# Cross-attention on one core: row maxima transposed on VectorE in 32x32 blocks, weight-by-value products in two blocks of four quads, four exponential buffers

## The reference, cut to what matters

```python
q = apply_axial_rope(q, pos_map)
k = apply_axial_rope(k, ctx_pos_map)
logits = jnp.einsum('bqhd,bkhd->bhqk', q, k) * scale
w = jax.nn.softmax(logits, axis=-1)
attn = jnp.einsum('bhqk,bkhd->bqhd', w, v)
```

## Time and profile before

| | |
|---|---|
| timed runs | 456.71 us median of 3 (454.82 to 458.28) |
| span of the profiled execution | 458.8 us |
| PE busy | 359.8 us (78%) |
| DVE busy | 244.2 us (53%) |
| ACT busy | 211.2 us (46%) |
| POOL busy | 167.2 us (36%) |

### The profile page before, as it was taken

How to read it: one execution, slowest core, us unless ns; L and a number is a source line. 1 busy time by engine, 2 the same in 40 slices (tenths; PEclk the granted TensorE clock), 3 DMA queues, 4 the chain that set the end, 5 groups by cost and what they waited for, 6 DMA issues and landing times. The chain is left out here.

```text
span 458.8 us, 9423 instructions
## 1 busy us (share of the span) xinstructions
PE 359.8 (78%) x3050; PEld 213.1 (46%) x3050; DVE 244.2 (53%) x654; ACT 211.2 (46%) x394; POOL 167.2 (36%) x241
## 2 busy tenths in 40 slices
PE   0545989999999999999999759876998898766000
PEld 0432546666666666666565424453546643322000
DVE  6364546766666676666767344799784430111000
ACT  2232557667666666666667375441662321111000
POOL 9144214442234443224300020242387142667730
PEclk9995899999999999999999857999999998697555
DMA  8896356101111000111320023411043787222245
GB/s 206 257 251 186 102 143 203 26 9 29 29 29 29 24 17 18 29 29 25 89 59 2 2 95 117 166 24 46 1 123 114 220 237 193 22 28 26 26 79 116
DMA packets 35036, 39.28 MB, mean 86 GB/s; under 512 B 8032, under 2 KB 29120, under 8 KB 34752
## 3 DMA queue, kind: packets, MB, share of 16 engines
q1 hardware_dynamic: 24082, 21.55, 16.5%
q10 hardware_dynamic: 8030, 11.93, 9.0%
q0 software_dynamic: 2896, 5.44, 7.0%
HBM read 26.36 MB, written 10.32 MB: 80 GB/s over the span
## 5 line engine op out<-in xcount | busy, mean ns | idle before, releaser
L469 DVE TENSOR_REDUCE mx<-bank 128x4 f16<-128x512 f32 x128 | 88.2, 690 | 45.6 <-PE bank L571 43.0
L364 ACT ACTIVATE pw<-bank 128x512 f32<-128x512 f32 x128 | 76.7, 599 | 56.8 <-PE bank L584 56.7
L244 POOL TENSOR_TENSOR rot<-t 128x256 f32<-128x256 f32 x30 | 21.2, 727 | 131.6 <-DVE t L462 131.6
L571 PE MATMUL bank<-kz,qst 128*128 128x512 f16 x128 | 50.6, 397 | 5.8 <-DMA kz<-kT 5.7
L597 PE MATMUL bank<-pw,V 128*32 128x128 f32 x1024 | 54.8, 286 | 0.1
L584 PE MATMUL bank<-qst,kz 128*128 128x128 f16 x512 | 50.1, 221 | 4.2 <-DMA qst<-mxs 4.2
L584 PEld LDWEIGHTS bank<-qst,kz 128*128 128x128 f16 x512 | 37.8, 99 | 14.6 <-issue 5.8
L597 PEld LDWEIGHTS bank<-pw,V 128*32 128x32 f32 x1024 | 20.2, 108 | 31.9 <-issue 30.4
L1171 PE MATMUL mbank<-hT,WSG 128*128 128x512 f16 (+1 forms) x144 | 32.6, 384 | 0.0
L873 POOL DMA_INDIRECT out<-ac,dst x16 | 21.7, 1355 | 29.6 <-DVE ac L1114 10.4
L1114 DVE TENSOR_SCALAR ac<-mbank,wpair 128x256 f32<-128x256 f32 x16 | 7.7, 484 | 45.7 <-DMA odd<-ac,dst 42.8
(11 more groups left out here) (174 smaller groups left out, 659.4 us busy)
## 6 DMA issues: line engine op xcount, KB each, us to landing
ring_gu<-in_L_ffn_w_gate_up ACTq DMA_DIRECT2D x20, 352.0 KB
kz<-kT SPq DMA_DIRECT2D x64, 64.0 KB, 2.0
ring_dn<-in_L_ffn_w_down ACTq DMA_DIRECT2D x10, 352.0 KB
ring_gu<-in_L_ffn_w_gate_up SPq DMA_DIRECT2D x8, 352.0 KB
X<-in_x SPq DMA_DIRECT2D x4, 512.0 KB, 7.3
table<-ac SPq DMA_DIRECT2D x8, 256.0 KB, 2.1
odd<-zero SPq DMA_DIRECT2D x1, 2048.0 KB, 7.0
out<-X SPq DMA_DIRECT2D x4, 512.0 KB, 3.1
```

The costliest lines, as they stand in the source:

```text
L244: eng.tensor_tensor(rot[:, part], t1[:, part], t2[:, part], ALU.add).then_inc(rot_ok[w], 1)
L364: act.activation(pw[g % 2][:, :], STB[g % 2][:, :], ACT.Exp, scale=SCALE).then_inc(exp_ok, 1)
L469: dve.tensor_reduce(mx[u // 2 % 2][:, :, u % 2], SB[u % 2][:, :].rearrange("p (j t) -> p j t", j=4), axis=AX.X, op=ALU.max, negate=True).t ...
L571: pe.matmul(SB[u % 2][:, :], qst[m.par][:, u, :], kz[m.par][:, :, u, :], start=True, stop=True).then_inc(s_mm, 1)
```

## The change

- `mx` becomes a tile of 128 x 32, of which 8 columns are written, the rest is zeroed once. DVE transposes it in 32x32 blocks straight into `mxs` (also 128 x 32). Each group of 32 tokens then has its 8 rows of maxima in its own 32 partitions. The PE transpose, its semaphore `mxT_mm`, and the copy from PSUM are gone.
- SP copies each half into `qst` with four DMAs, one for each group of 32 tokens (8 rows of 32 values), in place of one (8 rows of 128 values).
- `weigh_values` is called in two blocks: in step 4 for quads 0 to 3 of b, and in step 0 for quads 4 to 7 of b-1. Before, each step had one quad.
- The exponentials go to four buffers `pw`, so that four can wait.

```diff
                         sp.wait_ge(mxs_ok, k + 1)
-                        sp.dma_start(qst[who.par][MAXROW:P:SLOT, 2 * half:2 * half + 2, :],
-                                     mxs[half % 2][:, :]).then_inc(mr_in[half % 2], 16)
+                        for c in range(4):
+                            sp.dma_start(qst[who.par][MAXROW:P:SLOT, 2 * half:2 * half + 2, 32 * c:32 * c + 32],
+                                         mxs[half % 2][32 * c:32 * c + 8, :]).then_inc(mr_in[half % 2], 16)
...
-                        at_least(act, pv_mm, QUADS * b.n + g - 1)
-                        act.activation(pw[g % 2][:, :], STB[g % 2][:, :], ACT.Exp, scale=SCALE).then_inc(exp_ok, 1)
+                        at_least(act, pv_mm, QUADS * b.n + g - 3)
+                        act.activation(pw[g % 4][:, :], STB[g % 2][:, :], ACT.Exp, scale=SCALE).then_inc(exp_ok, 1)
...
-            def evac_max(m, half):
-                k = 4 * m.n + half
-                dve.wait_ge(mxT_mm, k + 1)
-                at_least(dve, mr_in[half % 2], 16 * (2 * m.n + half // 2))
-                dve.tensor_copy(mxs[half % 2][:, :], SB[1][0:8, 0:P // 2].bitcast(F16)).then_inc(mxs_ok, 1)
+            def turn_max(m, half):
+                dve.wait_ge(max_ok, QUADS * m.n + 2 * half + 2)
+                at_least(dve, mr_in[half % 2], 64 * (2 * m.n + half // 2))
+                dve.transpose(mxs[half % 2][:, :], mx[half % 2][:, :]).then_inc(mxs_ok, 1)
...
-            def transpose_max(m, half):
-                pe.wait_ge(max_ok, QUADS * m.n + 2 * half + 2)
-                pe.transpose(SB[1][0:8, 0:P // 2].bitcast(F16), mx[half % 2][:, :, :], identh[:, :]).then_inc(mxT_mm, 1)
...
-                    if g % 2 == 1:
-                        who, half = (b, (g + 3) // 2) if g < 5 else (m1, (g - 5) // 2)
-                        if inside(who):
-                            transpose_max(who, half)
...
                     if g == 0 and inside(o):
-                        weigh_values(o, QUADS - 1)
-                    if g > 0 and inside(b):
-                        weigh_values(b, g - 1)
+                        for q in range(4, QUADS):
+                            weigh_values(o, q)
+                    if g == 4 and inside(b):
+                        for q in range(4):
+                            weigh_values(b, q)
```

More of the change, by code:

```diff
@@ L179, in attention @@
         V = [sb(f"V{i}", [P, NH, SLOT]) for i in range(2)]
-        mx = [sb(f"mx{i}", [P, 4, 2], F16) for i in range(2)]
-        mxs = [sb(f"mxs{i}", [8, P], F16) for i in range(2)]
-        pw = [sb(f"pw{i}", [P, 4 * P]) for i in range(2)]
+        mx = [sb(f"mx{i}", [P, SLOT], F16) for i in range(2)]
+        mxs = [sb(f"mxs{i}", [P, SLOT], F16) for i in range(2)]
+        pw = [sb(f"pw{i}", [P, 4 * P]) for i in range(4)]
         OT = [sb(f"OT{i}", [P, 4, P]) for i in range(2)]
@@ L204, in attention @@
         consts, consts2, kz_zero = sem("consts"), sem("consts2"), sem("kz_zero")
+        mx_zero = sem("mx_zero")
         stat1, mv1_ok, std1, rs1_ok = sem("stat1"), sem("mv1_ok"), sem("std1"), sem("rs1_ok")
@@ L213, in attention @@
         v_mm, v_ok = sem("v_mm"), sem("v_ok")
-        s_mm, max_ok, mxT_mm, mxs_ok = sem("s_mm"), sem("max_ok"), sem("mxT_mm"), sem("mxs_ok")
+        s_mm, max_ok, mxs_ok = sem("s_mm"), sem("max_ok"), sem("mxs_ok")
         mr_in = [sem(f"mr_in{i}") for i in range(2)]
@@ L415, in _ @@
                                       ALU.mult, ALU.add).then_inc(turn_s, 1)
+            for i in range(2):
+                dve.memset(mx[i][:, :], 0.0).then_inc(mx_zero, 1)
             dve.wait_ge(turn_s, 4)
@@ L447, in _ @@
             statistics(0, 4, 0)
+            dve.wait_ge(mx_zero, 2)
             dve.wait_ge(rope_tab, 3)
@@ L466, in row_max @@
                 dve.wait_ge(s_mm, QUADS * m.n + u + 1)
-                if not (isinstance(m.n, int) and 4 * m.n + u // 2 < 2):
-                    dve.wait_ge(mxT_mm, 4 * m.n + u // 2 - 1)
-                dve.tensor_reduce(mx[u // 2 % 2][:, :, u % 2], SB[u % 2][:, :].rearrange("p (j t) -> p j t", j=4),
+                at_least(dve, mxs_ok, 4 * m.n + u // 2 - 1)
+                dve.tensor_reduce(mx[u // 2 % 2][:, u % 2:8:2], SB[u % 2][:, :].rearrange("p (j t) -> p j t", j=4),
                                   axis=AX.X, op=ALU.max, negate=True).then_inc(max_ok, 1)
-            def evac_max(m, half):
-                k = 4 * m.n + half
-                dve.wait_ge(mxT_mm, k + 1)
-                at_least(dve, mr_in[half % 2], 16 * (2 * m.n + half // 2))
-                dve.tensor_copy(mxs[half % 2][:, :], SB[1][0:8, 0:P // 2].bitcast(F16)).then_inc(mxs_ok, 1)
+            def turn_max(m, half):
+                dve.wait_ge(max_ok, QUADS * m.n + 2 * half + 2)
+                at_least(dve, mr_in[half % 2], 64 * (2 * m.n + half // 2))
+                dve.transpose(mxs[half % 2][:, :], mx[half % 2][:, :]).then_inc(mxs_ok, 1)
             def normalise(m, half):
@@ L499, in period @@
                         if inside(who):
-                            evac_max(who, half)
+                            turn_max(who, half)
                     who, u = (b, g + 5) if g < 3 else (m1, g - 3)
@@ L568, in logits_q @@
                 at_least(pe, max_ok, QUADS * m.n + u - 1)
-                if u % 2:
-                    at_least(pe, mxs_ok, 4 * m.n + u // 2)
                 pe.matmul(SB[u % 2][:, :], qst[m.par][:, u, :], kz[m.par][:, :, u, :], start=True, stop=True).then_inc(s_mm, 1)
-            def transpose_max(m, half):
-                pe.wait_ge(max_ok, QUADS * m.n + 2 * half + 2)
-                pe.transpose(SB[1][0:8, 0:P // 2].bitcast(F16), mx[half % 2][:, :, :], identh[:, :]).then_inc(mxT_mm, 1)
             def logits_k(m, g):
@@ L581, in logits_k @@
                     half = g // 2
-                    pe.wait_ge(mr_in[half % 2], 16 * (2 * m.n + half // 2 + 1))
+                    pe.wait_ge(mr_in[half % 2], 64 * (2 * m.n + half // 2 + 1))
                 for j in range(4):
@@ L597, in weigh_values @@
                     ins = pe.matmul(OB[g // 4][32 * j:32 * j + 32, (g % 4) * P:(g % 4) * P + P], V[m.par][:, 4 * g + j, :],
-                                    pw[g % 2][:, j * P:j * P + P], start=True, stop=True, tile_position=(0, 32 * j))
+                                    pw[g % 4][:, j * P:j * P + P], start=True, stop=True, tile_position=(0, 32 * j))
                 ins.then_inc(pv_mm, 1)
```

## The result

The changed kernel takes 473.78 us (median of 6 runs, 472.22 to 478.81), the kernel before 456.77 in the same runs: a ratio of 1.040 (95% interval 1.034 to 1.046), 17.0 us slower. The profiled execution has a span of 477.1 us, in a run of 478.81, the slowest of the six. The span before was 458.8.

A forecast was written before the change was run, and what follows sets the result against it. The prediction took a circle from SP's DMA issues through PE, ACT and DVE to bind at 14.60 us a batch; +9.6 over ten batches, +7.2 in the tail and +4 at the start gave 477 us, range 458 to 488.

The forecast's parts named there:

- circle: Way from SP's queue through PE, ACT and DVE back to SP: 14.60 us a batch, 0.96 more than now.
- Step 4: PE from step 4 to step 5 with a block of four quads: 2.09 us, where one quad took 1.26.
- ACT's part: From step 5's logits_k through the exponential, evac_OT and the copy to attnT, with the signal to PE: 1.80 us.
- the X addition: From project_out on PE to DVE's addition on X: 1.28 us.
- the way to SP: From the X addition through the maxima on DVE to SP: 0.57 us.
- The step from half 1 to the next kz: On SP, half 1's other three issues and the step to the next kz: 1.86 + 0.84 = 2.70 us.
- half 3 hide behind half 2: Way over half 3's landing lets project_out start at 9.85 us, against 10.05 over half 2, so it hides.
- The start: Before 85 us, three more issues in each PE wait for mxs DMAs: +4 us (2 to 8).
- The tail: From 221.90 us to the last project_out: 14.6, 14.4, 11.6 and 6.6, 47.2 us in all, +7.2.
- The clock rival: PE's granted clock falls as it idles 3 of 14.6 us: over 500 us; clock or another wait, chance 0.05.
- Cheap issues: Rival: SP's DMA issues are cheap and PE sets the end, 428 to 457 us; chance 0.12.
- Blocks that save nothing: Rival: a quad costs 0.47 us inside a block too, step 4 is 0.54 longer, 484 us; chance 0.06.

The follow-up runs named there:

- maxima first: The changed kernel with DVE's step 7 turned round, the transpose of half 1's maxima ahead of the X addition: 463.20 us, ratio 1.015.
- transposes-alone kernel: The changed kernel with weigh_values back at one quad a step and two buffers, keeping VectorE transposes and four DMAs a half: 480.52 us, 1.053 against the kernel before.
- one DMA a half: The changed kernel with only the first of each half's four mxs DMAs, leaving out the maxima of 96 of 128 tokens: 429.38 us, ratio 0.939.
- four-DMAs-alone kernel: The kernel before with each mxs DMA cut into four pieces of 32 tokens and nothing else: 479.32 us, ratio 1.052.
- kernel with kz on ACT: The changed kernel with its four kz DMAs a batch issued from ACT in place of SP: 459.52 us, ratio 1.009.
- blocks alone: The kernel before with only the two blocks of four quads and four exponential buffers: 436.98 us, ratio 0.957.

## Why the prediction was right

**What bounds.** That PE's idle-free list would give way to a circle from SP through PE, ACT, DVE and back was right, and shown from four sides: cutting the DMAs alone (+23 us), taking them away one by one, taking the ACT link out (-10.6 us), and taking kz off SP's queue (to 459.5 us from ACT, to 446.7 from GpSimd with the maxima first).

**Terms of the circle.** Forecast 14.60 us a batch, measured 14.1 in the eight of ten batches at full clock. From issue to issue it is 0.57 to 0.60 us where I took 0.62: 0.14 to 0.35 too much over seven. The extra dimension and the 64-byte rows cost nothing, the issue itself has 0.52 in the median where the one of 256-byte rows had 0.57:

```profile
L294 SPq DMA_DIRECT2D qst<-mxs x159: 520/521/599, 84.5 to 224.9; - x159
```

From the first issue of half 2 to `logits_k` it was 3.38 against 3.56. Step 4 was 1.83 against 2.09, because a further quad in a block costs less: 32 matmuls take 1.01 us to the next start (160.66 to 161.67) where eight take 0.36, thus 0.22 each, my lower bound, not 0.28. ACT's part was 1.83 against 1.80, the X addition 1.28 and the way to SP 0.57, as forecast. The VectorE transpose takes 0.20. The step from half 1 to the next kz was 2.36 where the loop doesn't turn, against 2.70 for the mean. All these misses made the forecast too slow: a batch was to lose 0.96 us and lost 0.46.

**Two ways in one circle.** I had half 3 hide behind half 2 by 0.2 us. In the trace they are as near: `logits_k` of step 6 waits 0.19 us for half 3, and then `project_out` 0.3 for ACT. In the transposes-alone kernel, which has a quad in that place, half 3 wins, and there my sum was 0.5 us a batch too low. I had kz land before step 3 needs it badly; from 85 to 236 us PE waits for it there ten times, 0.9 to 1.9 us each. In the batch shown it then waits 1.16 us more for half 2, so kz isn't the last.

**Start and tail.** The start cost 6.9 us, not 4, within 2 to 8. PE's waits for mxs DMAs from 20 to 85 us grew from 4.2 to 10.1:

```profile
PE bank L581 <- DMA qst<-mxs: 10.1, 5, 3.5
```

These waits alone don't explain it. With one DMA a half they are 8.9 us, and that kernel reaches its second `project_out` at 82.69, earlier than the kernel before. The clock is another part: before 92 us the changed kernel has three stretches at half clock, 14 us in all, that neither the kernel before nor the one with one DMA has. Here are the changed kernel and the one with one DMA:

```profile
50.00:92.00 42.00, 31.39 (x350) 23.06 (x348) 20.77 (x49) 20.59 (x38) 11.53 (x22) 0.84 0.41 121
```

```profile
50.00:92.00 42.00, 35.97 (x477) 27.47 (x479) 27.34 (x66) 28.41 (x51) 14.44 (x27) 1.00 0.45 129
```

The tail is 47.26 us, forecast 47.2, but that is luck. Its four parts are 15.58, 15.02, 10.81 and 5.85, where I had 14.6, 14.4, 11.6 and 6.6. The first two hold a stretch at half clock each, 6.8 us together.

**The clock rival** happened in small. Behind 50 us, its stretches in the attention are 3 to 7 us long, two of them in the ten batches:

```profile
91.00:131.00 40.00, 32.51 (x396) 24.71 (x395) 25.09 (x59) 25.47 (x46) 13.32 (x26) 1.00 0.10 25
131.00:135.00 4.00, 4.00 (x51) 3.01 (x48) 1.81 (x5) 1.85 (x4) 1.91 (x4) 0.57 0.06 14
135.00:203.00 68.00, 55.16 (x683) 42.01 (x680) 42.28 (x101) 42.56 (x77) 22.10 (x42) 1.00 0.10 24
203.00:207.00 4.00, 4.00 (x50) 3.10 (x50) 1.91 (x5) 1.94 (x4) 2.11 (x4) 0.57 0.04 10
```

PE was busy 32.5 of 40 us before the first fall, with no wait over 1.2 us, and the clock was back at 1.00 after it. The batches with a fall took 15.06 and 15.62 us in place of 14.1, together 2.5 us. So the ten batches' +7.1 are 4.6 of circle and 2.5 of clock. At the same 1.2 us a fall, an estimate, the tail's +7.3 are 4.8 of circle and 2.5 of clock. My sum had 9.6 + 7.2 = 16.8 for these two, all of it circle; at full clock it would have been about 9.4. The circle's mechanism was right, but its cost was put nearly twice too high, and the clock, which the sum left out, made up part of the difference. The clock never stayed low, so the 500 us of that rival were far off.

**The other rivals.** Cheap issues: no, 0.52 and more for each. The section "Anatomy of one DMA" of the Trainium skill's page "DMA: Bandwidth & Descriptors" would have had the sequencer nearly free of them; the measurement decides against reading it so for SP. GpSimd's own queue was held 0.50 us by each kz DMA; how much of that is the sequencer's dispatch no row shows. Blocks that save nothing: no (by my terms step 4 would be 4 x 0.47 - 1.30 = 0.58 us longer, not 0.54); the blocks alone gave 1.48 us a batch, where my sum of single edits had 1.16.

## What to carry to other kernels

Count what each sequencer issues in a round, and not only what each engine computes: here a DMA that was cut into four cost three more issues of nearly the old price, each with a quarter of the bytes, and no busy column shows them. When two edits come together, price each alone. Here the blocks were worth 20 us and the transposes with their four DMAs cost 24, and 17 slower is more than their sum, since what the blocks free on PE can't be had while the circle binds. In a list of instructions in order, what is needed by the slow way round goes ahead of what waits for something else: turning round two DVE instructions gave back 10.6 us.

## What I had not expected of the hardware

The issue of the same kz DMA (SBUF to SBUF) took 0.59 us on SP, 0.68 on ACT and 0.50 on GpSimd, in the medians of the ten batches. GpSimd's, which the profile books under `software_dynamic`, was the quickest, and it landed as soon as SP's: 1.9 us in the median against 2.0.

The clock fell for a few us in the changed kernel with PE busy four fifths of the time and no wait over 1.4 us in the 68 us before the second fall, and didn't from 78 to 262 us in the kernel with kz on ACT, busy 106 of 120:

```profile
95.00:215.00 120.00, 106.07 (x1322) 79.17 (x1320) 77.94 (x190) 79.74 (x148) 43.32 (x81) 1.00 0.11 26
```

It didn't fall in the ten batches of the four-DMAs-alone kernel either, where a batch takes 14.4 us as well, but PE is busy 133.48 of 140. What decides stays open; no run here was made to tell.
